# A graph network on one core: in the GINE layers the gathers of a group are issued only once the rows of the group before have landed

## The reference

```python
for l in range(3):
    e = edge_attr @ W_lin[l] + b_lin[l]
    msg = relu(x[src] + e)
    agg = segment_sum(msg, dst, num_segments=n)
    h = x + agg
    h = relu(h @ W1[l] + b1[l]) @ W2[l] + b2[l]
    x = relu(batch_norm(h) * gamma[l] + beta[l])
```

## Time and profile before

| what | value |
|---|---|
| time, median of 3 runs | 5072.95 us (5072.32 to 5081.31) |
| the profiled execution's own time | 5085.52 us |
| its span, first to last instruction | 5083.7 us |
| mean granted TensorE clock | 0.784 of full speed |
| gathers of line 986 | 1176, in three passes from 1837 to 3919 us |
| busy in the span | TensorE 70%, VectorE 52%, GpSimd 50%, ScalarE 32% |

### The profile page before, as it was taken

One profiled execution on the slowest core, in us unless ns is written; L12 is line 12 of the kernel. 1 busy time (PEld: TensorE's weight loads), 2 busy tenths in 40 slices (PEclk: granted clock), 3 DMA queues, 4 the chain that ended last, 5 costly groups with the idle time before them and its releaser, 6 DMA issues. The chain is left out here.

```text
span 5083.7 us, 91413 instructions
## 1 busy us (share of the span) xinstructions
PE 3545.7 (70%) x20792; PEld 2661.7 (52%) x20793; DVE 2651.7 (52%) x6184; ACT 1604.4 (32%) x3137; POOL 2542.1 (50%) x2650
## 2 busy tenths in 40 slices
PE   6999999777777634554635555455555699999997
PEld 3666666544444424443424444244444578787874
DVE  6777777745555532332322232323323677777775
ACT  3566666544444421111201111111112433333334
POOL 3555555356666655555365555355553344444440
PEclk7999999889999955555655555655556899999998
DMA  3333333222222211111111111111111333333330
GB/s 104 94 92 93 92 93 93 73 57 65 66 67 67 65 46 49 53 51 51 46 51 52 51 53 52 47 51 51 52 52 35 94 96 100 95 100 95 101 94 16
DMA packets 293250, 349.78 MB, mean 69 GB/s; under 512 B 63536, under 2 KB 236755, under 8 KB 292915
## 3 DMA queue, kind: packets, MB, share of 16 engines
q0 software_dynamic: 98528, 229.12, 16.0%
q1 hardware_dynamic: 140481, 92.05, 6.5%
q10 hardware_dynamic: 54162, 27.77, 1.9%
HBM read 332.61 MB, written 16.07 MB: 69 GB/s over the span
## 5 line engine op out<-in xcount | busy, mean ns | idle before, releaser
L986 POOL DMA_INDIRECT gath<-source_rows_narrow,gine_idx x1176 | 1127.1, 958 | 925.7 <-SPq L967 488.5
L1000 PE MATMUL psum<-gine_lin,ea 32*128 32x128 f32 x2928 | 290.2, 486 | 1034.9 <-DVE vs L1034 969.9
L1064 ACT ACTIVATE pm<-vs 128x512 f32<-128x512 f32 x366 | 230.5, 630 | 1809.1 <-DVE vs L1034 1548.6
L1000 PEld LDWEIGHTS psum<-gine_lin,ea 32*128 32x128 f32 x2928 | 185.1, 299 | 1137.1 <-DVE vs L1034 910.4
L1140 POOL DMA_INDIRECT gath<-source_rows,idx_all x416 | 428.9, 1031 | 636.6 <-DVE vs L1261 452.2
L1009 PE MATMUL psum<-hot,pm 128*128 128x128 f32 x2928 | 730.0, 428 | 8.5 <-ACT pm L1064 8.3
L760 POOL DMA_INDIRECT gath<-source_rows,idx_all x488 | 469.0, 961 | 433.1 <-PE psum L807 318.2
L1034 DVE TENSOR_TENSOR vs<-psum,gath 128x512 f32<-128x512 f32 x366 | 253.2, 692 | 820.6 <-remote 518.3
L1009 PEld LDWEIGHTS psum<-hot,pm 128*128 128x128 f32 x2928 | 626.9, 316 | 91.2 <-ACT pm L1064 53.9
L760 POOL DMA_INDIRECT gath<-source_rows_narrow,idx_all x488 | 462.0, 947 | 329.5 <-remote 140.3
L790 PE MATMUL psum<-lk,att_b 128*128 128x512 f32 x732 | 403.7, 638 | 123.1 <-issue 67.9
(11 more groups left out here) (238 smaller groups left out, 5631.0 us busy)
## 6 DMA issues: line engine op xcount, KB each, us to landing
rel<-rel_rows SPq DMA_DIRECT2D x244, 128.0 KB
ea<-in_edge_attr_tiles SPq DMA_DIRECT2D x416, 64.0 KB
ea<-in_edge_attr ACTq DMA_DIRECT2D x366, 64.0 KB
gath<-source_rows_narrow,gine_idx POOLq DMA_INDIRECT x1176
gath<-source_rows,idx_all POOLq DMA_INDIRECT x904
rel<-quad_rel_rows SPq DMA_DIRECT2D x104, 128.0 KB
gath<-source_rows_narrow,idx_all POOLq DMA_INDIRECT x488
source_rows<-ACC SPq DMA_DIRECT2D x12, 512.0 KB, 2.9
```

What stands on the lines that cost most here:

```text
L986: pool.indirect_dma_start(out=ring[:, g % RING, j, :], out_offset=None, in_=table1, in_offset=bass.IndirectOffsetOnAxis(ap=gine_idx[:, g, ...
L1000: last = e.matmul(E[:, j, :], ea[rows, s, :], gine_lin[rows, layer, :], start=True, stop=True)
```

## The change

On GpSimd, ahead of the four gathers of each group but the first, the kernel now waits until all four gathers of the group before have landed.

```diff
                 def _(pool):
                     pool.wait_ge(gine_idx_in, 16)
                     for g in range(GROUPS):
+                        if g:
+                            pool.wait_ge(gi_gath[(g - 1) % RING], landings((g - 1) % RING, (g - 1) // RING))
                         if g >= RING:
                             pool.wait_ge(gi_free, layer * GROUPS + g - RING + 1)
                         for j in range(SUBS):
```

## The result

| | before | after |
|---|---|---|
| median of 5 runs each | 5072.95 us (5068.91 to 5083.07) | 5048.64 us (5046.14 to 5049.58) |
| after / before, 95% interval | | 0.9949 (0.9936 to 0.9962) |
| the three passes | 678.7, 670.8, 676.7 us | 674.4, 664.1, 663.8 us |

The passes run from the first gather to the end of the last addition to `ACC`. They lose 2026.2 - 2002.3 = 23.9 us, near the 24.3 us between the medians; forecast were 103. (The two profiled executions lie 36.5 us apart by their spans, 5083.7 and 5047.2.

A forecast was written before the change was run, and what follows sets the result against it. VectorE, late through TensorE's results while gathers are dense, was taken as the bound. 97 x 6.50 + 6.5 + 4.05 gives 641.1 us a pass, three 1923 against 2026, 103 less: 4970 us, range 4865 to 5110.

The forecast's parts named there:

- the chain issue, landing, issue: On GpSimd after the change: each group's issues, then their landing, then the next issues set the pace, 6.50 us a group.
- What bounds before: In the three passes VectorE is late through TensorE's results while gathers are dense; 992 of 2026 us are "remote" waits.
- The pause: GpSimd's added wait for a group's last gather to land: taken as 1.75 us, within 0.30 us of 1.69.
- The four issues, 4.75 us: GpSimd's issuing of a group's four gathers takes 377.02 / 98 + 3 x 0.30 = 4.75 us.
- VectorE keeps up: After the change VectorE isn't late and the ring never full: 5.2 us an item needed, 3.4 allowed by such bursts.
- a silence that outlasts the landing: Ahead of a GpSimd burst: pauses of 1.75 us and more let two VectorE items through, those up to 1.40 didn't.
- the 18 short pauses: GpSimd pauses of 1.28 to 1.40 us in the earlier trace; VectorE's second item came 6.3 to 8.6 us into the burst.
- One item per burst: Rival, chance 0.18: TensorE's results stay stuck all burst, VectorE does one item per 6.50 us; slower, up to 5427 us.
- the wait comes on top: Rival, chance 0.05: landing delay and VectorE's lateness add up, 142 us a pass, 426 in all; slower, 5499 us.
- No change: Rival, chance 0.08: VectorE stays at 5.5 us an item whatever the bursts' shape; time within some 13 us of 5073.
- its bound for the period, 6.74: Longest forecast time from one group's gathers to the next group's, in a span 6.14 to 6.74 us; it gives 5040 us.

The follow-up runs named there:

- e2: Kernel before with iota in PSUM and two GpSimd fills ahead of each group (silence 1.39 us), no landing wait: 4857.58 us, ratio 0.9558.
- p4: Kernel before with iota in PSUM and one small GpSimd fill ahead of every gather, no landing wait: 4844.16 us, ratio 0.9526.
- b1: Kernel before with iota copied to PSUM for the hot line, no wait added: 5153.91 us, ratio 1.0025.
- c1: Changed kernel with the wait one group further back, for the group before the last: 5176.38 us, ratio 1.0074.
- a1: Changed kernel with iota copied to PSUM each pass, so the hot line reads one SBUF input: 5020.34 us, ratio 0.9756.
- e1: Kernel before with iota in PSUM and one GpSimd fill ahead of each group (silence 0.81 us), no landing wait: 5038.52 us, ratio 0.9901.
- h1: Kernel before without gathers; SyncE loads each group in one plain transfer, always the table's first 512 rows: 4177.08 us in one run.
- p1: Kernel before with two GpSimd fills ahead of each group, iota left in SBUF, no landing wait: 4867.44 us, ratio 0.9581.
- q1: Kernel before with iota in PSUM and a 96-column GpSimd fill ahead of every gather, no landing wait: 5013.94 us, ratio 0.9866.

## Why the prediction was wrong, point by point

The forecast was 4970 us, in a range from 4865 to 5110; measured were 5048.64. The direction held, and so did the chain issue, landing, issue that the sum follows; the gain was 24 us for 103. The step that failed is the term of 4.75 us for a group's four issues.

- **What bounds before**: held. VectorE was late through TensorE's results while gathers were dense; 992 us of "remote" went when the gathers were thinned out, by the change and by e2 and p4 alike (2, 63 and 4 us), while b1 and c1, which don't thin them, keep them (1067 and 1043 us in the three passes). The granted clock doesn't tell them apart: 0.53 in before's first pass, 0.54 in p4's.
- **The pause**: 1.75 was taken, 1.77 measured. The 1.69 us from the end of the last issue to the use in the earlier trace rows carried over.
- **The four issues, 4.75 us**: this is the term that was mis-sized. It was read from the earlier trace rows, where gathers start at any time with respect to VectorE, and 35 in 1176 met the `hot` line. The added wait ties both engines to one landing, and 203 meet it. Measured were 5.06, 4.94 and 4.94; (0.31 + 0.19 + 0.19) x 97 = 67 us, and the pause's 0.02 x 291 = 6, make most of the 79 us between forecast and result. a1, which removes this alone, has passes of 645 us for the forecast's 641, on another chip and with a pause of 1.83. The trace of before showed it already: its 35 long gathers were hidden in the mean of 958 ns.
- **VectorE keeps up**: held. 11 items in the first 63 us for the 12 that were named, no wait of line 967 left.
- **The condition, a silence that outlasts the landing**: fell with e2 and p4. So VectorE's keeping up was forecast rightly from a wrong condition. What the 18 short pauses of before were is not shown; the likelier reading is that pause and lateness had one cause, the dense gathers, and I read the one as the cause of the other.
- **One item per burst**, and **the wait comes on top**: neither occurred. The first rested on that same condition, and its 0.18 with it. **No change** was near in size (24 us for its 13), but not in cause.
- The range held the time, but not by the forecast's own case: 5048.64 lies above its 4865 to 5040, and its bound for the period, 6.74, was passed in the first pass (6.83).

**What stays open.** Why TensorE's results reach VectorE late when gathers are issued at more than one per 1.49 us: no trace records what they wait for. The semaphore updates in the traces narrow it to TensorE's own side. In before, `e_ready`, which counts line 1000's products, goes up 2.0 us after their recorded end in the median and up to 25 us after, and the count of line 1009's 0.8 us and up to 23; the counts of VectorE's and ScalarE's lines follow their ends within 0.02 us, in before, after, e1, e2, p4 and h1 alike. In h1 TensorE's counts, too, come within 0.05 us. So what comes late is TensorE's, not SyncE's word or VectorE's own work. Whether the products end late or only the count is, this can't tell, since the recorded ends of products are modelled. h1 excludes only the rate of bytes. A kernel without any gathers, with GpSimd at other work, was not tried, nor one with gathers of fewer rows, which would tell a limit by instructions from one by rows.

**The best version** is p4, evenly spaced gathers with `iota` in PSUM: 4844.16 us, 0.9526 of before, where the change gives 0.9949. e2, at 0.9558 on another chip, can hardly be told from it.

## What to carry to other kernels

If an engine is late for a release that the profile can't name, thin out what GpSimd issues and look for the fastest rate at which it isn't late: here two fills ahead of each group gave eight times the gain of waiting for its landing (p1's 0.9581 for 0.9949). A wait that releases two engines by one event also fixes where their next instructions meet; list which of them read SBUF twice before you take the durations of free-running engines for the new order. A mean duration hides a second mode: split a group's instructions by length and by what runs beside them before you multiply.

## What the runs showed that I had not expected

- A gather of 128 rows that begins 0.07 to 0.30 us after a VectorE line of 0.69 us with two SBUF inputs ends 1.50 to 1.52 us after that line's start, so most take 1.37 us for 0.94. If it begins within 0.03 us of the line's start or before it, or if one of the inputs is in PSUM, it takes 0.94 to 0.95 (after, a1).
- TensorE's semaphore counts can lag its recorded products by 2.0 us in the median and 25 us at most while the other engines' follow within 0.02 us (before).
- A small step in the rate decides: from 1.41 to 1.49 us per gather VectorE's waits for anything but SyncE fall from 1306 to 490 us, the waits for the ring end, and the ratio goes from 0.9866 to 0.9526 (q1, p4), with 1.43 to 1.46 in between (0.9821 to 0.9659).
- With plain loads for gathers, the same engines do an item in 3.1 us and the kernel takes 4177 us: the gathers cost before some 900 us, though GpSimd, which issues them beside the other engines, has time to spare (h1, one run).
